# Squared norms in attention: GpSimd's add of the two halves is taken out, and VectorE's reduction reads all 64 columns of each head

## What is computed

```python
xn = _ln(x, ln_scale)
Q = einsum('bse,hef->bhsf', xn, W_q)      # 8 heads of 64 columns; K and V likewise
q2 = sum(Q * Q, axis=-1)[..., :, None]
k2 = sum(K * K, axis=-1)[..., None, :]
sqdist = maximum(q2 + k2 - 2.0 * einsum('bhsf,bhtf->bhst', Q, K), 0.0)
scores = exp(-gamma * sqdist)
out = einsum('bhst,bhtf->bhsf', scores, V)
```

## Time and profile before

| | |
|---|---|
| runs | 873.78 us median of 3 (871.83 to 874.65) |
| profiled execution | 871.59 us, span 869.0 us |
| mean granted TensorE clock | 0.982 |
| busy share of the span | TensorE 88%, VectorE 81%, GpSimd 60%, ScalarE 57% |

### The profile page before, as it was taken

One profiled execution on the slowest core, in us unless ns is written; L12 is line 12 of the kernel. 1 busy time (PEld: TensorE's weight loads), 2 busy tenths in 40 slices (PEclk: granted clock), 3 DMA queues, 4 the chain that ended last, 5 costly groups with the idle time before them and its releaser, 6 DMA issues.

```text
span 869.0 us, 16981 instructions
## 1 busy us (share of the span) xinstructions
PE 766.4 (88%) x5712; PEld 438.4 (50%) x5712; DVE 702.2 (81%) x1810; ACT 491.1 (57%) x913; POOL 519.9 (60%) x719
## 2 busy tenths in 40 slices
PE   1699979999999999999999999899889899998894
PEld 1234346666666666666666665344344344444341
DVE  5376768999999999999999998577787877777652
ACT  0365668877887887888788785232333333333221
POOL 7260255445445344454454452469999999999867
PEclk9999979999999999999999999899999999999997
DMA  4300021111221112211112210000000000000000
GB/s 113 136 16 2 1 49 38 36 38 38 49 50 27 39 35 50 50 41 33 38 38 50 49 33 18 1 2 7 8 7 8 7 7 14 7 8 7 8 7 18
DMA packets 22789, 25.71 MB, mean 30 GB/s; under 512 B 12816, under 2 KB 21648, under 8 KB 22576
## 3 DMA queue, kind: packets, MB, share of 16 engines
q1 hardware_dynamic: 22384, 23.85, 11.5%
q10 hardware_dynamic: 320, 0.79, 0.4%
HBM read 5.30 MB, written 2.43 MB: 9 GB/s over the span
## 4 chain that ended last, share of the span: by engine, by line
PE 43%; DVE 33%; POOL 11%; issue 5%; ACT 3%; DMA 2%; SPq 1%; another core or an unknown queue 1%; POOLq 0%; DVEq 0%; ACTq 0%
DVE prob L753 15%; DVE m L769 9%; PE bank L1034 6%; PE bank L962 6%; PE bank L1149 6%; PE bank L1169 6%; PE bank L1082 5%; POOL cxn L425 5%; PE bank L1058 3%; PE bank L1060 2%; DVE qk L763 2%; POOL gated L436 2%; DVE wtok L877 2%; POOL cinv L421 2%; PE bank L1160 2%
## 5 line engine op out<-in xcount | busy, mean ns | idle before, releaser
L753 DVE TENSOR_SCALAR prob<-prob,cap_hi,cap_lo 125x250 f32<-125x250 f32 x512 | 232.7, 502 | 18.6 <-ACT prob L531 15.8
L401 POOL TENSOR_TENSOR sq<-sq 125x256 f32<-125x256 f32 x128 | 96.3, 759 | 170.7 <-ACT sq L545 126.7
L884 DVE SCALAR_TENSOR_TENSOR gated<-bank,nb,wb 128x500 f32<-128x500 f32 x160 | 115.7, 732 | 71.7 <-PE bank L1149 66.4
L1169 PE MATMUL bank<-gated,w_sb 64*64 64x500 f32 x1024 | 172.8, 594 | 0.0
L1149 PE MATMUL bank<-cs,w_sb 64*64 64x500 f32 x1024 | 170.4, 587 | 0.4 <-DVE gated L884 0.4
L531 ACT ACTIVATE prob<-bank 125x500 f32<-125x500 f32 x256 | 148.6, 591 | 38.0 <-PE bank L1060 35.0
L602 ACT ACTIVATE relu<-bank,b_sb 128x500 f32<-128x500 f32 x96 | 65.0, 678 | 175.1 <-PE bank L1149 170.5
L436 POOL TENSOR_TENSOR gated<-relu,wb 128x500 f32<-128x500 f32 x96 | 125.0, 1307 | 48.0 <-ACT relu L602 48.0
L1034 PE MATMUL bank<-prob,u 125*64 125x250 f32 x1024 | 125.8, 382 | 1.5
L1058 PE MATMUL bank<-m,s 128*125 128x500 f32 x256 | 111.0, 434 | 6.1 <-issue 6.1
L1060 PE MATMUL bank<-m,s 112*125 112x500 f32 x256 | 101.0, 395 | 0.0
(11 more groups left out here) (165 smaller groups left out, 1371.8 us busy)
## 6 DMA issues: line engine op xcount, KB each, us to landing
m<-m SPq DMA_DIRECT2D x128, 125.0 KB, 2.3
out<-res SPq DMA_DIRECT2D x16, 125.0 KB
xa<-xparts SPq DMA_DIRECT2D x4, 281.2 KB
w_sb<-in_w SPq DMA_DIRECT2D x1, 1024.0 KB
xw<-xparts SPq DMA_DIRECT2D x4, 140.6 KB
w_sb<-in_w SPq DMA_DIRECT2D x1, 512.0 KB
m<-s SPq DMA_DIRECT2D x32, 15.6 KB
xparts<-x_part SPq DMA_DIRECT2D x1, 375.0 KB, 4.0
```

Source lines behind the costliest of these rows:

```text
L753: last = dve.tensor_scalar(part, part, cap_hi[0:T, h:h + 1], cap_lo[0:T, h:h + 1], ALU.min, ALU.max)
L884: dve.scalar_tensor_tensor(gated[g % 8][:, :], up_bank(g)[:, 0:C], nb1[:, g:g + 1], wb[q % 2][:, :], ALU.max, ALU.mult).then_inc(c_gated, 1)
L1169: last = pe.matmul(y[cols, 0:C], w2_sb[rows, g, :], gated[g % 8][rows, :], start=g == 1 and rows is HI, stop=v == 7, skip_group_check=True)
```

## The change

GpSimd's loop over the eight units goes, with the `sq2` buffers. VectorE's reduction reads the squares themselves, 64 columns of each head instead of 32, as soon as ScalarE has written them (semaphore `b_ev`). ScalarE's wait for a free `sq` buffer is on VectorE's reduction of unit k-2 (`b_red`) instead of on GpSimd's add of unit k-2 (`b_sum`). The place of the reductions and of the squares in their engines' programs stays.

```diff
-        m1, s2, u_sb, sq, sq2, prob, y_att = phase(
+        m1, s2, u_sb, sq, prob, y_att = phase(
...
-            ("sq2_", 2, [T, H, D // 2], F32),
...
                 if new:
-                    for k in range(8):
-                        q = k % 2
-                        gp.wait_ge(b_ev, 16 * p + k + 1)
-                        wait(gp, b_red, 8 * p + k - 1)
-                        gp.tensor_tensor(sq2[q][:, :, :], sq[q][:, :, 0:D // 2], sq[q][:, :, D // 2:D], ALU.add)\
-                            .then_inc(b_sum, 1)
                     gp.wait_ge(b_red, 8 * p + 8)
...
                     elif k < 8:
-                        wait(act, b_sum, 8 * p + k - 1)
+                        wait(act, b_red, 8 * p + k - 1)
                         act.activation(sq[k % 2][:, :, :], src[0:T, :].rearrange("p (h d) -> p h d", h=H), ACT.Square)\
                             .then_inc(b_ev, 1)
...
-                        dve.wait_ge(b_sum, 8 * p + n + 1)
-                        dve.tensor_reduce(qk[:, n // 2, n % 2, :], sq2[n % 2][:, :, :], AX.X, ALU.add)\
+                        dve.wait_ge(b_ev, 16 * p + n + 1)
+                        dve.tensor_reduce(qk[:, n // 2, n % 2, :], sq[n % 2][:, :, :], AX.X, ALU.add)\
                             .then_inc(b_red, 1)
```

## The result

The changed kernel takes 965.58 us (median of 4 runs, 963.14 to 965.68), against 872.81 us for the kernel before in the same comparison: 1.106 times as long, 95% interval 1.1022 to 1.1099. The forecast was 961 us, the range 930 to 990. The span of the profiled execution goes from 869.0 to 962.8 us, 93.8 us more.

The account below looks back on a forecast made before the run. The prediction took attention steps to be bound by nearly full TensorE and VectorE. 871.6 us profiled plus 73.5 for the loop and 14.4 for clock falls gave 959.5; with the median 2.2 higher it said 961, range 930 to 990.

Parts of the forecast that it names:

- The busy time is an even trade: VectorE in attention: caps without adds beside them give back 2.3 us per step, longer reductions add 2.1 us.
- A sum by it alone: Attention steps by the shared-port rule only: 15 x (2.1 - 2.3) = -3 us, giving 869 us.
- The loop: ScalarE's squares and VectorE's caps and reductions take turns in attention: 4.9 us more per step, 73.5 us over 15.
- A turn: From one ScalarE exponential's start to the next, through caps, reduction and square: 2.53 us.
- The hop from VectorE to ScalarE: From a reduction's end to the square waiting for it: 0.09 us, lower bound 0.04.
- no slack behind the last reduction: After each step's last reduction nothing absorbs the delay, since VectorE and TensorE are both full.
- The clock: TensorE's clock falls for lack of work in 12 of 15 attention steps, 1.2 us each, 14 us; bounds 0 and 30.
- rival 2: The loop with longer clock falls on TensorE, each costing twice 2 us: 1005 us at most, about 985; chance 0.10.
- The 2.2 us: Added to the forecast because the median of the runs stood that far above the profiled execution.
- That the clock holds: Rival: the loop forms in attention but TensorE's clock does not fall, 947 us; chance 0.25.
- The gain by a freed VectorE: Rival: ScalarE never waits for reductions, VectorE saves 0.85 us per attention step, 13 us, giving 861 us; chance 0.07.

Follow-up runs that it names:

- run 8: Changed kernel with four sq buffers and GpSimd's eight adds put back into buffers nobody reads, squares also waiting for them: 881.88 us, 1.0111 times the kernel before.
- run 1: Changed kernel with four sq buffers instead of two, square k waiting for reduction k-4: 873.71 us, 1.0017 times the kernel before.
- run 3: Changed kernel with 12 matmuls added per step in TensorE's two long gaps, their result overwritten by the transposes: 945.96 us, 1.0846 times the kernel before.
- run 5: Changed kernel with four sq buffers and VectorE's reductions one unit earlier in its program: 863.0 us, 0.9892 times the kernel before.
- run 6: Kernel before with VectorE's reductions one unit earlier alone, adds and two sq buffers kept: 862.26 us, 0.9873 times the kernel before.
- run 7: Changed kernel, still two sq buffers, with VectorE's reductions one unit earlier alone: 870.86 us, 0.9965 times the kernel before.

## Why the prediction was right

**The busy time is an even trade: right, and beside the point.** A reduction was put at 0.67 us and is 0.678. Over 16 pairs the reductions take 34 us more and the caps 36 us less, 2.15 and 2.3 us per step where 2.1 and 2.3 were expected. The rule on the shared port in the page "SBUF — State Buffer" of the Trainium skill, "Who interferes with whom", holds in run 8: caps beside adds take longer, and a reduction takes 674 ns there against 678 in the changed kernel. A sum by it alone gave 869 us, and run 1, without the loop, is at 873.7. One reading of the prediction was loose, with nothing resting on it: the cap of 291.91 ended at 292.72, 0.15 us after the add and not with it.

**The loop: right, link by link.** A turn was put at 2.53 us and is 2.54. From the caps of slot (1,1) to the end of the last reduction 17.54 us were expected; the timeline has 310.18 + 0.68 - 293.34 = 17.52. The lengthening of a step was put at 4.9 us and is 31.33 - 26.49 = 4.84. The hop from VectorE to ScalarE, taken from GpSimd's, is 297.29 - 297.20 = 0.09. That no slack behind the last reduction takes any of it up was right as well: at full clock the two steps differ by what the loop adds.

**The clock: right in kind, too cheap.** A fall in 12 of 15 steps at 1.2 us each, 14 us, was expected. Each fall comes at the end of a loop and is paid in the stretch behind it. Of the 15 loops, 11 of the first 14 have one, which costs 17.4 us in the steps, and the last loop has the twelfth, 2.6 us (below). So the number was right, and the mis-sized term is the price: 20 us for 12 falls, 1.7 us each. In four of the steps the granted clock was 0.90 on the mean and the step 2.3 us longer, the longer falls of rival 2; the others, at 0.94 or 0.95, cost 1.0 to 1.3.

**Behind the last reduction: 4.1 us.** The clock is low there too, where the last loop leads into the next stage:

```profile
604.17:611.00 6.83, 5.96 (x20) 4.20 (x22) 6.17 (x13) 4.48 (x8) 5.40 (x8) 0.51 0.27 59
```

```profile
514.48:521.00 6.52, 5.65 (x34) 4.07 (x35) 6.30 (x14) 5.22 (x11) 5.51 (x8) 1.00 0.25 56
```

The first is of the changed kernel, the second the same place before. In run 3, which has no fall there, the stretch behind the last reduction is shorter than in the changed kernel: 944.7 - 588.70 = 356.0 us against 962.8 - 604.17 = 358.6; before it was 869.0 - 514.48 = 354.5. So 2.6 of the 4.1 us go with the fall that run 3 avoids; the other 1.5 were not foreseen and not followed up.

**The sum, and some luck in it.** The loops cost 67.8 us in 14 steps and 4.6 up to the end of the first, 72.4 where 73.5 were expected; the falls cost 20 where 14.4 were expected. The terms gave 959.5 us for a profiled execution that took 965.49. The 2.2 us that were added because the median stood so far above the profiled execution before (959.5 + 2.2 is 961.7, said as 961) did not come again: the median after stands 0.1 above. They made up for part of the falls, so the forecast is nearer the median, 4.6 us, than its terms are.

**The rivals.** That the clock holds (947 us) is what run 3 brought about: 946. The gain by a freed VectorE (861 us) needed two things that the change doesn't have, a wait that doesn't close a loop and an earlier last reduction; with both (run 5) it is 863, and the adds need not go for it (run 6).

## What to carry to other kernels

When a buffer's release moves from one engine to another, look at where the releasing instruction stands in its new engine's program, and what stands ahead of it: if that depends on something behind the waiting instruction's predecessor, two engines that overlapped take turns, and no sum of busy times shows it. Here either the release one place earlier in program order (run 7) or more buffers (run 1) undid it. And in a ring through several engines it pays to look for an instruction that others wait for behind work that nobody needs yet: putting it ahead was worth 1.3% in the kernel before (run 6).

## What the runs showed of the hardware that was not expected

Adding matmuls made the kernel faster: with 12 more of them per step the granted clock stayed at 1.00 and the time went from 965.58 to 945.96 us. The price of a fall varied with how long it lasted: steps with a mean granted clock of 0.94 or 0.95 were 1.0 to 1.3 us longer than those at 1.00, steps with 0.90 were 2.2 to 2.4 us longer. And of the 15 loops, all with two matmuls between two gaps of 1.4 to 1.8 us at their end, 12 were followed by a fall and three were not.
